# Plain 32-bit matmuls in place of three rounded passes, in a two-layer macaron network

## What is computed

```python
x = x + 0.5 * L0_ffn(layernorm(x))     # "layers": depth 2, see below
x = x + L0_attn(layernorm(x))          # causal linear attention, 16 heads of 16
x = x + 0.5 * L0_ffn(layernorm(x))
x = x + 0.5 * L1_ffn(layernorm(x))     # ternary: weights are -1, 0 or 1
x = x + L1_attn(layernorm(x))          # gated attention, k'v per sequence
x = x + 0.5 * L1_ffn(layernorm(x))

def L0_layer(x):                       # twice in each L0_ffn, own weights
    q, k, v = split(shift_token(x) @ wqkv)          # 256 -> 3 x 512, 8 heads of 64
    q, k = rotary(l2norm(q) * qs, l2norm(k) * ks)
    x = x + local_attention(q, k, v) @ wo           # window 128 and the one before
    h = layernorm(shift_token(x)) * lg + lb
    a, g = split(h @ w1 + b1)                       # 256 -> 2 x 682
    return x + (a * gelu(g)) @ w2 + b2              # 682 -> 256
```

## Time and profile before

| | |
|---|---|
| median of 3 runs | 3722.87 us (3719.95 to 3725.91) |
| profiled execution: time, span | 3722.95, 3721.1 us |
| TensorE matmuls busy | 3329.4 us, 89% |
| VectorE, ScalarE, GpSimd busy | 2576.0, 1774.7, 1568.1 us |
| mean granted TensorE clock | 0.964 of full speed |

### The profile page before, as it was taken

How to read it: one execution, slowest core, us unless ns; L and a number is a source line. 1 busy time by engine, 2 the same in 40 slices (tenths; PEclk the granted TensorE clock), 3 DMA queues, 4 the chain that set the end, 5 groups by cost and what they waited for, 6 DMA issues and landing times.

```text
span 3721.1 us, 77570 instructions
## 1 busy us (share of the span) xinstructions
PE 3329.4 (89%) x26336; PEld 2753.0 (74%) x26468; DVE 2576.0 (69%) x5542; ACT 1774.7 (48%) x4415; POOL 1568.1 (42%) x1536
## 2 busy tenths in 40 slices
PE   1999989979999898997899998979999896886779
PEld 0777768857777787886677777857777685775668
DVE  4777767667777675776677767767777676765567
ACT  1666652246666323543566662236666421442235
POOL 3777750067777102333677760047777200113220
PEclk9999989989999999998999999999999998999999
DMA  4000011010000111000100002110000110000001
GB/s 148 11 15 15 13 36 49 23 40 14 15 15 16 37 31 44 10 10 15 34 15 13 15 15 65 28 41 14 15 15 12 52 34 10 23 0 0 0 7 40
DMA packets 146259, 93.52 MB, mean 25 GB/s; under 512 B 19644, under 2 KB 142872, under 8 KB 145432
## 3 DMA queue, kind: packets, MB, share of 16 engines
q1 hardware_dynamic: 146072, 91.07, 8.2%
HBM read 49.08 MB, written 25.17 MB: 20 GB/s over the span
## 4 chain that ended last, share of the span: by engine, by line
PE 35%; POOL 32%; issue 26%; DVE 5%; ACT 1%; DMA 1%; POOLq 1%; DVEq 0%; SPq 0%; ACTq 0%
POOL prob L2273 11%; POOL rn L2260 10%; POOL qk L2267 6%; PE bank L279 5%; PE bank L280 5%; PE bank L281 5%; PE bank L559 2%; PE bank L558 2%; PE bank L592 2%; PE bank L591 2%; PE bank L599 2%; PE bank L598 2%; PE bank L597 2%; PE bank L548 1%; PE bank L691 1%
## 5 line engine op out<-in xcount | busy, mean ns | idle before, releaser
L2273 POOL TENSOR_TENSOR prob<-prob,rsum 128x512 f32<-128x512 f32 x512 | 523.9, 1043 | 266.8 <-DVE rsum L1544 266.8
L1009 ACT ACTIVATE prob<-bank,nmax 128x256 f32<-128x256 f32 x1024 | 474.2, 481 | 138.2 <-DVE nmax L1538 138.2
L1538 DVE TENSOR_REDUCE nmax<-bank 128x2 f32<-128x512 f32 x512 | 340.2, 687 | 207.1 <-PE bank L386 207.1
L2267 POOL TENSOR_TENSOR qk<-rot_t 128x512 f32<-128x512 f32 x256 | 324.3, 1288 | 298.0 <-DVE ss L1518 298.0
L2243 POOL TENSOR_TENSOR rstd<-meanvar,eps 128x4 f32<-128x4 f32 x48 | 11.2, 233 | 909.0 <-DVE meanvar L1479 909.0
L1169 ACT ACTIVATE gate<-bank,bias 128x512 f32<-128x512 f32 x192 | 132.5, 690 | 544.3 <-PE bank L281 544.2
L2260 POOL TENSOR_TENSOR rn<-ss,mhalf 128x16 f32<-128x16 f32 x128 | 375.3, 2932 | 10.7
L279 PE MATMUL bank<-wqkv_hi,hT_hi 128*128 128x512 f32 x768 | 340.8, 444 | 28.6 <-DVE qT_lo L1532 11.0
L1017 ACT ACTIVATE probT<-bank 128x512 f32<-128x512 f32 x512 | 310.7, 611 | 116.3 <-PE bank L403 115.7
L279 PE MATMUL bank<-gT_hi,w_hi 128*128 128x512 f32 x704 | 280.8, 399 | 31.2 <-DVE w_lo L1645 31.2
L281 PE MATMUL bank<-wqkv_hi,hT_lo 128*128 128x512 f32 x768 | 307.3, 400 | 0.0
(11 more groups left out here) (276 smaller groups left out, 9307.1 us busy)
## 6 DMA issues: line engine op xcount, KB each, us to landing
ya<-Y SPq DMA_DIRECT2D x40, 256.0 KB, 2.3
H<-Y SPq DMA_DIRECT2D x128, 64.0 KB, 1.8
H<-ya SPq DMA_DIRECT2D x128, 64.0 KB, 1.8
yb<-Y SPq DMA_DIRECT2D x128, 64.0 KB, 1.6
HB<-Y SPq DMA_DIRECT2D x32, 256.0 KB, 2.8
HB<-yb SPq DMA_DIRECT2D x32, 256.0 KB, 3.0
raw<-in_L_ffn_wqkv SPq DMA_DIRECT2D x4, 1536.0 KB, 6.3
raw<-in_L_ffn_w SPq DMA_DIRECT2D x4, 1364.0 KB, 6.0
```

Source lines behind the costliest of these rows:

```text
L1009: ins = e.activation(Pb[gi][:, i * 256:(i + 1) * 256], bk[:, i * 256:(i + 1) * 256], ACT.Exp, bias=nm[r][:, x:x + 1], accum_out=sums[r][:, ...
L1538: e.tensor_reduce(nm[r][:, 2 * gi:2 * gi + 2], bk[:, :].rearrange('p (h k) -> p h k', h=2), AX.X, ALU.max, negate=True).then_inc(s_dvMX[gi ...
L2267: e.tensor_tensor(half(u, j), t1[:, w], t2[:, w], ALU.add).then_inc(s_plAD[j], 1)
L2273: e.tensor_tensor(pair, pair, rs[:, 2 * gi:2 * gi + 2].unsqueeze(2).to_broadcast([P, 2, 256]), ALU.mult).then_inc(s_plPN[gi], 1)
```

## The change

All products that went through `three`, and those with two products in the feed-forward layers, become one plain 32-bit matmul on unsplit operands. Scores stay split. The low tiles, the copies and subtractions that made them, and the semaphores between are gone: a copy by ScalarE (or the product on VectorE) writes the operand that TensorE reads. Weights are loaded by DMA straight into the tiles that are used (`w1`, `w2`, `wq`, `wo`, `wa`, `wp`, `wgates`, `Wa`, `Wb`), with w1's four pieces in four DMAs. What `prep_A` did at every pass in memsets is done once (`first_values`), and the rotary tables are multiplied at the end of the stage before (`rotary_tables`). In the ternary feed-forward ScalarE alone makes the hidden tile, in a ring of four, and `w2` follows two chunks behind and not three. In the gated one the last two chunks of `w2` both stand behind the first chunk of the next group.

```diff
-            def three(o, lh, ll, rh, rl, start, stop):
-                e.matmul(o, lh, rh, start=start, stop=False)
-                e.matmul(o, lh, rl, start=False, stop=False)
-                return e.matmul(o, ll, rh, start=False, stop=stop)
...
-                        i = three(o, hTh[u % 2][:, lt], hTl[u % 2][:, lt], wq_h[w], wq_l[w], k == 0, k == KD - 1)
+                        i = e.matmul(o, hT[u % 2][:, lt], wq[w], start=k == 0, stop=k == KD - 1)
...
-                        i = three(bank[7][:, 0:D], OTh[:, lt], OTl[:, lt], wo_h[:, c, :], wo_l[:, c, :], c == 0, c == KI - 1)
+                        i = e.matmul(bank[7][:, 0:D], OT[:, lt], wo[:, c, :], start=c == 0, stop=c == KI - 1)
...
-                nch, LAG, TRAT = (CH, 2, 3) if l0 else (CF, 3, 5)
+                nch, LAG, TRAT = (CH, 2, 3) if l0 else (CF, 2, 5)
...
-                        if l0:
-                            i = three(o, w1_h[w], w1_l[w], hi[:, k, :], lo[:, k, :], k == 0, k == KD - 1)
-                        else:
-                            e.matmul(o, w1_h[w], hi[:, k, :], start=k == 0, stop=False)
-                            i = e.matmul(o, w1_h[w], lo[:, k, :], start=False, stop=k == KD - 1)
+                        i = e.matmul(o, w1[:, k, col:col + P], gT[par][:, k, :], start=k == 0, stop=k == KD - 1)
...
-                            e.matmul(o, hidh[:, c % RING, lt], w2_h[:, c, :], start=False, stop=False, skip_group_check=True)
-                            i = e.matmul(o, hidl[:, c % RING, lt], w2_h[:, c, :], start=False, stop=last, skip_group_check=True)
+                            i = e.matmul(o, hid[:, c % RING, lt], w2[:, c, :], start=False, stop=last, skip_group_check=True)
...
-                            e.matmul(o, hidh[:, c, lt], w2_h[:, c, :], start=opens, stop=False, skip_group_check=True)
-                            e.matmul(o, hidh[:, c, lt], w2_l[:, c, :], start=False, stop=False, skip_group_check=True)
-                            i = e.matmul(o, hidl[:, c, lt], w2_h[:, c, :], start=False, stop=False, skip_group_check=True)
+                            x = hidt[:, lt] if last else hid[:, c, lt]
+                            i = e.matmul(o, x, w2[:, c, :], start=opens, stop=last, skip_group_check=True)
...
-            def ot_(T, u):
-                G = R0 + T
-                e.wait_ge(s_acOT, G + 1 + OFF)
-                e.tensor_tensor(OTl[:, :], bank[6][:, :], OTh[:, :].bitcast(F32), ALU.subtract).then_inc(s_dvOT, 1)
...
+            def first_values():
+                e.memset(w1[:, :, 2 * MAIN:], 0.0).then_inc(s_prepB, 1)
+                e.memset(w2[:, CH - 1, :], 0.0).then_inc(s_prepB, 1)
+                e.memset(hidt[:, :], 1.0).then_inc(s_prepB, 1)
+                e.memset(kTh[:, :, :, :].bitcast(F32), 0.0).then_inc(s_prepB, 1)
+                e.memset(kTl[:, :, :, :].bitcast(F32), 0.0).then_inc(s_prepB, 1)
+                e.memset(V[U - 1][:, :], 0.0).then_inc(s_prepB, 1)
+                e.tensor_copy(mask0[:, :], maskE).then_inc(s_prepB, 1)
...
+                if l0 and pas % DEPTH < DEPTH - 1:
+                    rotary_tables()
...
-                e.dma_start(raw[:, :].rearrange('p (k n) -> p k n', k=KD), a['L0_ffn_wqkv'][one, :, :].rearrange('a (k p) n -> p (a k) n', p=P)).then_inc(s_raw, 16)
+                e.dma_start(wq[:, :, :], a['L0_ffn_wqkv'][one, :, :].rearrange('a (k p) n -> p (a k) n', p=P)).then_inc(s_raw, 16)
```

More of the change, by code:

```diff
@@ L40, with tables_ready @@
 LAST0 = (CH - 1) * GRP * NRUN
+MAIN = (CH - 1) * P
+NINIT, NROT, NLIN = 7, 6, 8
+def tables_ready(run):
+    return NINIT + NROT * (run + 1) + (NLIN if run >= DEPTH else 0)
 OFF = 16
@@ L225, in build @@
         y1 = [sb(f"y1_{i}", [P, D]) for i in range(2)]
-        y1h = [sb(f"y1T_hi{i}", [P, D], F32R) for i in range(2)]
-        y1l = [sb(f"y1T_lo{i}", [P, D], F32R) for i in range(2)]
+        y1T = [sb(f"y1T{i}", [P, D]) for i in range(2)]
         scope.pop().close()
@@ L611, in group @@
                             tr(n + 1)
-                        if c >= LAG:
+                        if l0 and c < LAG:
+                            if c == 0 and not first:
+                                w2_(n - 1, CH - 2, 1 - par)
+                                w2_(n - 1, CH - 1, 1 - par)
+                        elif c >= LAG:
                             w2_(n, c - LAG, par)
@@ L804, in of_tile @@
                         x = (slice(None), k, slice(t * P, (t + 1) * P))
-                        i = three(o, h1h[x], h1l[x], w[0][:, k, :], w[1][:, k, :], k == 0, k == KD - 1)
+                        i = e.matmul(o, h1[x], w[:, k, :], start=k == 0, stop=k == KD - 1)
                     return i
@@ L834, in q @@
                             wc = (slice(None), k, slice(c * P, (c + 1) * P))
-                            ins = three(o[:, :], wqg2[0][wc], wqg2[1][wc], h1h[:, k, w], h1l[:, k, w], k == 0, k == KD - 1)
+                            ins = e.matmul(o[:, :], wqg[wc], h1[:, k, w], start=k == 0, stop=k == KD - 1)
                         ins.then_inc(g_peQ, 1)
@@ L874, in pr @@
                         lt = slice(k * P, (k + 1) * P)
-                        i = three(o, y1h[r][:, lt], y1l[r][:, lt], wog2[0][:, k, :], wog2[1][:, k, :], k == 0, k == KD - 1)
+                        i = e.matmul(o, y1T[r][:, lt], wog[:, k, :], start=k == 0, stop=k == KD - 1)
                     i.then_inc(z_pePR, 1)
@@ L1802, in gated_group @@
                             norm_rows(n + 1)
-                        if c == 3 and more:
-                            tr(n + 1, 1 - par)
                 def relu_group(n, par):
@@ L1808, in relu_group @@
                     more = not (isinstance(n, int) and n == GRP - 1)
[L1809 to L1822 removed]
+                    if more:
+                        ffn_stats(pas, l0, n + 1)
+                    if not first:
+                        w2_(n - 1, 1 - par, 0, U)
+                    if more:
+                        norm_rows(n + 1)
                 group = gated_group if l0 else relu_group
```

664 lines of the change are left out of this document (160 added, 504 removed).

## The result

The changed kernel takes 4237.7 us, median of four runs (4235.08 to 4241.64), against 3722.65 us for the kernel before: ratio 1.1384, interval 1.1364 to 1.1404. The prediction said 4263, range 4205 to 4345. The profiled execution took 4235.08 us, its span is 4233.3, so 512.2 us more than before's; the forecast was 540.

What follows compares the result with a forecast made beforehand. The prediction took TensorE's stream of columns to bound four of five stages. Stage terms of +603 us and borders of -63 gave +540 on 3722.95, so 4263 us, range 4205 to 4345 for 8 in 10.

Steps and rivals of the forecast that it cites:

- linear attention: Linear attention slot: two products of 512 columns and four of 256 turn plain, +0.67 us per slot, +21 over 32.
- gated attention: Gated attention: two 512-column products per tile less a switch, +9 us; q projection +6; u and output projections 0.
- gated attention's start and the rest: Gated attention's waits at its starts, -5 us; low parts of first transposed tile and attention output at stage ends, -5.
- The price: TensorE, per plain matmul: two records of two cycles per column plus 0.005 us, 0.864 us for 512 columns, 0.437 for 256.
- Rival 1: TensorE: a plain record costs what a rounded one does, 0.458 and 0.238 us per matmul; total 3112 us; chance 0.05.
- rival 2: TensorE: each plain record carries a rounded record's extra, adding 71 us for 4334; chance 0.12.
- rival 4: Feed-forward groups: long stretches of plain matmuls drop the clock to 1.2 GHz, total 5720 us; chance 0.02.
- The switch: Attention slot: longer spacing of the first rounded matmul after a transpose vanishes, three times: -0.25 us, bounds 0 and -0.35.
- The cover over the u and output products: Gated attention: four 256-column products' extra 0.32 us per tile fits TensorE's 0.88 us idle, costing 0; without cover +10.
- The borders: Stage borders and kernel start, where splitting stood on the path: -63 us in all, bounds -30 and -85.
- Rival 3: Stage borders: gains do not come because loads or GpSimd's tables take the splits' place; 4326 us; chance 0.06.
- VectorE's relief: Steady stretches: what VectorE and ScalarE lose is worth nothing, as TensorE's column stream sets four of five stages.

Runs made afterwards that it cites:

- Experiment 3: Kernel before with only the attention pass's out projection as one plain matmul on the high parts, low parts made but unused: 3761.57 us, ratio 1.0107.
- experiment 1: Kernel before with every two- or three-pass product replaced by one plain matmul on the high parts, all splits kept: 4321.73 us, ratio 1.1622.
- experiment 6: Kernel before with all rounded passes kept and only splits and rotary tables moved off the border paths: 3680.19 us, ratio 0.9895.
- experiment 7: As experiment 6, with GpSimd's key-tile clearing behind the first layer norm and its rotary tables after the last group's low parts: 3671.32 us, ratio 0.9866.
- experiment 4: Kernel before with only the high x high pass of every product, all splitting still done: 3194.51 us, ratio 0.8591.

## Why the prediction was right

What was claimed as the mechanism held: TensorE's stream of columns sets four of five stages, a plain product costs more than three rounded ones, and the borders give some back. That the sum came within 28 us is in part luck, since two steps missed by 30 us or so in opposite directions. By the prediction's own steps, the changes of the profiled execution, each from start to start of TensorE's records (a stage from its first transpose or product to its last product, an attention pass to the next stage's first transpose, a border from the last product to the first transpose):

| term | forecast | measured |
|---|---|---|
| attention passes | +144 | +135 |
| gated feed-forward, first product to last | +198 | +191 |
| ternary feed-forward, the same | +225 | +220 |
| linear attention | +21 | +13.4 |
| gated attention | +15 | +15 |
| attention to feed-forward, four | -26 | -27.2 |
| into attention, twice, and once behind the linear attention | -21 | -20.2 |
| start | -6 | -8.9 |
| gated attention's start and the rest | -10 | -6.6 |
| sum | +540 | +512 |

- The price: 0.864 and 0.437 us were taken, 0.859 and 0.432 measured. The 0.005 us per record was read from eight records of 128 columns, whose 0.111 took in the step to the next instruction; records behind each other are 0.109 apart. That is 1920 x 0.005 + 2048 x 0.005 = 20 us too much. Rival 1 (a plain record at a rounded one's price) and rival 2 (a rounded record's extra on each) fall by the same rows, and rival 4 by the clock of 1.00 in groups of 30 us.
- The switch: -0.25 us per slot was taken, 128 x 0.25 = 32 us. Experiment 3 shows it as a matter of where a start is recorded. The bounds given, 0 and -0.35, held it only near their end. This is a step that failed; it did not show in the sum, by luck, because another went the other way: the slot grew by 1.29 us (1.33 by the price), but only some 26 of the 32 intervals per pass are steady. While the pipeline fills, waits between engines take up part of the growth (in the first pass the first five intervals grew by 2.4 us together, not 6.5). In the second and third pass these five even shrank, by 1.1 and 1.3 us: the third interval fell from 13.95 to 11.07, and in the kernel before the clock is at 0.50 there (from 780.64 to 787.46 in the second pass). The last stretch, in which the pipeline drains, did not grow either (-0.7 to +0.4 us). So the passes came out 9 us below the forecast.
- The linear attention: its slot came as forecast (9.60), the stage 7.6 us under. With the splits kept it grew by 19.9 us (experiment 1), close to the forecast's 21; the other 6.6 came back with the change, 4.9 of them as busy time at a higher clock. The forecast had no term for this.
- The cover over the u and output products in the gated attention held: 2.72 us per tile. Its +15 came as forecast, but by luck: with the splits kept the stage grew by 22.7 us, and 7.7 came back with the change, 5.5 of them as busy time at a higher clock (experiment 1).
- The borders: -62.9 against -63. The start gave 2.9 us more than taken. The gated attention's start came as taken (-5.3 against -5), but its low parts and the rest, taken at -5, came to -1.3. Rival 3 falls. Experiments 6 and 7 gain 50 us (3721.43 - 3671.32, on one chip) with the rounded passes in place: most of the gain was in the order of splits, tables and clearing, not in the plain matmul. The 13 us between are mainly ahead of the gated feed-forward, where its first product comes 5.1 us behind the transposes in experiment 7 and 2.5 to 2.7 in the changed kernel.
- That VectorE's relief is worth nothing held in the steady stretches; outside them experiment 1 shows the whole of the preparation to be worth about 20 us more than the borders named, about half of it as time at a lower clock (4.9 and 5.5 us in two stages).

## What to carry to other kernels

Price a matmul by records and moving columns from its own start-to-start spacing over a run of equal records, never across a change of type: where TensorE is full, three rounded passes (0.69 us) beat one plain 32-bit matmul (0.86), and with exact weights two (0.46) beat it by far. When an edit bundles a dearer product with the removal of its preparation, ask which part of the gain needs the product: here 50 of 63 us came from waiting for each split only where it is first used and from moving tables and clearing off the border. A low pass that may be left out is the larger lever (-14% with all splits in place), but it gives up precision, and what comes next is VectorE's chain and a falling clock.

## What the runs showed of the hardware

- TensorE comes out of a border at 1.2 GHz. Before, behind an idle row of 7.37 us, records run at a granted clock of 0.50 from 552.61 to 558.72 and at 1.00 from 558.98 (first fence); after, behind one of 1.07 us, at 0.50 from 572.33 to 576.73 only (second fence). The mean clock of the whole rose from 0.964 to 0.979. So a border costs more than its idle row: work at half clock takes twice as long, which makes about 3 us of the 6.1 and 2.2 of the 4.4 (an estimate from these windows). Columns as in the earlier trace rows.

```profile
552.61:558.72 6.11, 6.11 (x14) 4.82 (x15) 0.50 (x1) 1.97 (x2) 0.00 (x0) 0.50 0.84 293
558.98:564.00 5.02, 5.02 (x25) 4.18 (x24) 4.57 (x13) 1.38 (x2) 1.21 (x2) 1.00 0.69 266
```

```profile
572.33:576.73 4.40, 4.40 (x5) 1.80 (x6) 0.00 (x0) 1.66 (x2) 0.00 (x0) 0.50 0.92 321
```

- In experiment 4's gated groups, where TensorE waits 4.3 and 4.5 us for VectorE, the granted clock is 0.77, and part of its 26.95 us of busy time is made of slow records (four that take 0.64 us elsewhere take 1.46 behind the wait): fewer passes gave less than their share.
- The first rounded record behind transposes is shown 0.08 us early, with the gap behind it longer by as much (0.20 us for 0.12, experiment 3).
- GpSimd and VectorE slow each other when VectorE reads two operands from SBUF: 0.69 to 1.67 us and 0.73 to 1.19 (experiment 6); a copy within SBUF went from 0.43 to 0.80. With these apart in experiment 7, the group is back from 25.17 to 24.12 us.
